# A gated tanh recurrence on TensorE: float16 split products replaced by float32 products in four column tiles

## What is computed

```python
h = silu(cond @ W1.T + b1)                       # layer 1 of the gate
gate = sigmoid(h @ W2.T + b2)[:, None, :]        # layer 2
... Haar transform of x along the steps, every coefficient times gate, inverse transform -> a
x = x + (x + a)
xW = einsum('ntd,dh->nth', x, Wx) + b
h_t = tanh(h_prev @ Wh + xW[t])                  # 256 steps in sequence, h0 = cond
x = x + h_t
```

## Time and profile before

| | before |
|---|---|
| median of 3 runs | 229.54 us (229.52 to 229.65) |
| the profiled execution | 229.55 us, of which span 227.8 us |
| PE busy | 223.4 us (98%), 3465 matmul records |
| weight loads (PEld) | 208.2 us, 3465 |
| DVE busy | 138.7 us (61%) |
| ACT busy | 108.2 us (48%) |

### The profile page before, as it was taken

The page is one execution under the profiler, slowest core; times in us unless marked ns, Lnnn a source line. Parts: engine busy times, 40 slices in busy tenths (PEclk is TensorE's granted clock), DMA queues, the critical chain, the costliest instruction groups (busy, mean ns, idle before and its releaser), DMA issues.

```text
span 227.8 us, 8577 instructions
## 1 busy us (share of the span) xinstructions
PE 223.4 (98%) x3465; PEld 208.2 (91%) x3465; DVE 138.7 (61%) x786; ACT 108.2 (48%) x773; POOL 0.5 (0%) x5
## 2 busy tenths in 40 slices
PE   7999999999999999999999999999999999999995
PEld 7899999999999999999999999999999999999984
DVE  3656666666666666666666666666666666666653
ACT  1344544455444554445544455444554445544452
POOL 0000000000000000000000000000000000000000
PEclk9999999999999999999999999999999999999999
DMA  6799930202020020202002020100202011020211
GB/s 190 219 398 415 406 140 12 86 0 98 3 92 3 3 92 4 96 3 92 3 3 94 4 95 0 77 21 4 94 3 95 0 53 45 4 94 3 95 46 49
DMA packets 6717, 18.41 MB, mean 81 GB/s; under 512 B 1171, under 2 KB 2454, under 8 KB 6678
## 3 DMA queue, kind: packets, MB, share of 16 engines
q1 hardware_dynamic: 6528, 17.71, 20.4%
q10 hardware_dynamic: 150, 0.15, 0.2%
HBM read 9.48 MB, written 8.39 MB: 78 GB/s over the span
## 4 chain that ended last, share of the span: by engine, by line
PE 97%; ACT 1%; DVE 0%; issue 0%; ACTq 0%; DVEq 0%
PE banks L241 58%; PE banks L232 33%; PE banks L221 3%; PE banks L207 2%; PE banks L215 1%; ACT L178 1%; ACT tanh_z L178 0%; ACT z L180 0%; DVE h_t L334 0%; DVE silu L359 0%; ACT h_t L198 0%; DVE ones L338 0%; DVEq L401 0%; ACTq L197 0%; ACTq L177 0%
## 5 line engine op out<-in xcount | busy, mean ns | idle before, releaser
L241 PE MATMUL banks<-h,wh_a 128*128 128x32 f16 x1530 | 132.8, 179 | 0.0
L392 DVE TENSOR_TENSOR h<-h_t,h 128x32 f16<-128x32 f32 x510 | 74.7, 188 | 81.0 <-ACT h_t L198 81.0
L232 PE MATMUL banks<-x,wx_sb 128*128 128x128 f32 x512 | 113.0, 305 | 0.0
L241 PE MATMUL banks<-h_t,wh_last 128*128 128x32 f32 x510 | 104.1, 286 | 0.0
L241 PE MATMUL banks<-h,wh_b 128*128 128x32 f16 x765 | 102.7, 176 | 0.0
L195 ACT ACTIVATE h<-banks 128x32 f16<-128x32 f32 x255 | 50.3, 197 | 110.1 <-PE banks L241 108.5
L241 PEld LDWEIGHTS banks<-h,wh_a 128*128 128x128 f16 x1530 | 86.1, 96 | 14.3
L232 PEld LDWEIGHTS banks<-x,wx_sb 128*128 128x128 f32 x512 | 75.9, 189 | 0.2 <-issue 0.2
L241 PEld LDWEIGHTS banks<-h_t,wh_last 128*128 128x128 f32 x510 | 75.8, 188 | 0.0
L241 PEld LDWEIGHTS banks<-h,wh_b 128*128 128x128 f16 x765 | 62.8, 97 | 0.0
L198 ACT ACTIVATE h_t<-banks 128x64 f32<-128x64 f32 x256 | 57.1, 223 | 0.8 <-PE banks L241 0.6
(11 more groups left out here) (33 smaller groups left out, 11.8 us busy)
## 6 DMA issues: line engine op xcount, KB each, us to landing
x<-in_x SPq DMA_DIRECT2D x15, 512.0 KB, 10.9
out_dram<-h_t SPq DMA_DIRECT2D x15, 512.0 KB, 2.6
x<-in_x SPq DMA_DIRECT2D x2, 256.0 KB, 5.0
wh_floor<-in_wh SPq DMA_DIRECT2D x1, 256.0 KB, 2.9
w_t<-in_w SPq DMA_DIRECT2D x1, 256.0 KB, 4.1
wx_sb<-in_wx SPq DMA_DIRECT2D x1, 256.0 KB, 4.9
out_dram<-h_t SPq DMA_DIRECT2D x1, 256.0 KB, 2.1
w_t<-in_w_cond SPq DMA_DIRECT2D x1, 145.0 KB, 2.6
```

What stands on the lines that cost most here:

```text
L232: return nc.tensor.matmul(pre[c % 2][e][m][:, steps, :], wx_sb[:, k, m * P:(m + 1) * P], moving, start=False, stop=False, skip_group_check ...
L241: return nc.tensor.matmul(pre[t // CS % 2][s % 2][m][:, s // 2, :], weights, h_part, start=start, stop=stop, skip_group_check=True)
L392: nc.vector.tensor_tensor(h2[:, t % 2, m, :], h_t[:, c, m, cols], h1[:, t % 2, m, :], ALU.subtract).then_inc(h2_ready[m], 1)
```

## The change

All products use PE as four tiles of 32 columns: `by_columns` cuts the 128 output columns of each weight block into four matmuls of 32 weight columns, each writing its own 32 partitions of PSUM. That holds for the gate, the bias, the input, the recurrence and the warm-ups. The recurrence is one float32 product for each of the four blocks, in the order k outside, m inside, with a wait for half k of h before each k. There are no float16 parts, no scale and nothing that computed it. ACT makes two tanhs a step, one for each half, straight into `h_t`. DVE makes no h2. A small tanh at the start loads ACT's table ahead of the gate; the gate's second layer is taken half by half, with warm-ups between; wh is loaded after wx; two bias products move behind the first input products; the last two steps are added and stored one by one.

The diff, cut to its core:

```diff
-        h1 = sb("h1", [P, 2, HALVES, B], F16)
-        h2 = sb("h2", [P, 2, HALVES, B], F16)
...
-        banks = [[ctx.enter_context(nc.psum_tensor(f"banks_{s}{e}", [P, HALVES, 512], F32)) for e in range(2)]
-                 for s in range(2)]
-        bank = [[[b[:, m, :] for m in range(HALVES)] for b in slot] for slot in banks]
+
+
+
+        bank = [[[ctx.enter_context(nc.psum_tensor(f"bank_{s}{e}{m}", [P, 512], F32)) for m in range(HALVES)]
+                 for e in range(2)] for s in range(2)]
         pre = [[[b[:, 0:N // 2].rearrange("p (s b) -> p s b", b=B) for b in parity] for parity in slot]
                for slot in bank]
 
-        scale_ps = bank[1][1][1][:, 256:257]
-        COPIES = 4
-        z_ps = [[bank[1][0][m][:, 256 + layer * P:256 + (layer + 1) * P].rearrange("p (n b) -> p n b", b=B)
-                 for m in range(HALVES)] for layer in range(2)]
+        z_ps = [[bank[1 - layer][layer][m][:, 256:256 + B] for m in range(HALVES)] for layer in range(2)]
...
-                   (CHUNKS - 1, 14, 2, T // 2)]
+                   (CHUNKS - 1, 14, 1, T // 2), (CHUNKS - 1, 15, 1, T // 2 + 1)]
...
             sp.dma_start(w1_t[:, 0, :], w1_cond[:, 0, :]).then_inc(w1_loaded[0], DMA)
-            sp.dma_start(wh_sb, wh).then_inc(wh_loaded, DMA)
             sp.dma_start(w2_t[:], w2).then_inc(w2_loaded, DMA)
             sp.dma_start(x1[:, 0, :, 0:FIRST], x[:, 0, :, 0:FIRST]).then_inc(x_first_loaded, DMA)
             sp.dma_start(wx_sb[:], wx).then_inc(wx_loaded, DMA)
+            sp.dma_start(wh_sb[:], wh).then_inc(wh_loaded, DMA)
             sp.dma_start(x1[:, 0, :, FIRST:N], x[:, 0, :, FIRST:N]).then_inc(x_loaded[0], DMA)
...
+            act.wait_ge(ones_ready, 1)
+            nc.scalar.activation(table_t[:], ones[:, 0:1], ACT.Tanh)
...
             for t in range(T):
                 c, s = t // CS, t % CS
-                z_t = banks[c % 2][s % 2][:, :, s // 2 * B:(s // 2 + 1) * B]
-                act.wait_ge(pre_ready[0], t + 1)
-                if t < T - 1:
-                    nc.scalar.activation(h1[:, t % 2, 0, :], z_t[:, 0, :], ACT.Tanh, scale=unscale_reg).then_inc(h1_ready[0], 1)
-
-                act.wait_ge(pre_ready[1], t + 1)
-                nc.scalar.activation(h_t[:, c, :, s * B:(s + 1) * B], z_t, ACT.Tanh,
-                                     scale=unscale_reg).then_inc(h_ready, 1)
-                if t < T - 1:
-                    nc.scalar.activation(h1[:, t % 2, 1, :], z_t[:, 1, :], ACT.Tanh, scale=unscale_reg).then_inc(h1_ready[1], 1)
+                for m in range(HALVES):
+                    act.wait_ge(pre_ready[m], t + 1)
+                    nc.scalar.activation(h_t[:, c, m, s * B:(s + 1) * B], pre[c % 2][s % 2][m][:, s // 2, :], ACT.Tanh)\
+                        .then_inc(h_ready[m], 1)
...
+            def by_columns(out, weights, moving, start=False, stop=False):
+                for q in range(0, P, 32):
+                    done = nc.tensor.matmul(out[q:q + 32], weights[:, q:q + 32], moving,
+                                            start=start, stop=stop, skip_group_check=True)
+                return done
...
+                return by_columns(pre[c % 2][e][m][:, steps, :], wx_sb[:, k, m * P:(m + 1) * P], moving)
...
+            def recur(t, k, m, h_part, start=False, stop=False):
+                return by_columns(pre[t // CS % 2][t % 2][m][:, t % CS // 2, :], wh_sb[:, k, m * P:(m + 1) * P], h_part,
+                                  start=start, stop=stop)
...
-            warm_up(23, bank[1][1][0])
-            gate_layer(0, w1_t, w1_t[:, :, D:D + B], z1_product, w1_loaded)
-            pe.wait_ge(small_ready, 1)
-            pe.wait_ge(largest_ready, 1)
-            nc.tensor.matmul(scale_ps, small[:], high_half(largest[:]), start=True, stop=True).then_inc(scale_product, 1)
-            warm_up(8, bank[1][1][0])
+            warm_up(22, bank[1][1][0])
+            for m in range(HALVES):
+                for k in range(HALVES):
+                    if m == 0:
+                        pe.wait_ge(w1_loaded[k], DMA)
+                    done = gate_product(0, k, m, w1_t, cond_t)
+                done.then_inc(z1_product, 1)
+            warm_up(6, bank[1][1][0])
             pe.wait_ge(w2_loaded, DMA)
-            pe.wait_ge(silu_ready, 1)
-            gate_layer(1, w2_t, silu2, z2_product, None)
+            for k in range(HALVES):
+                pe.wait_ge(silu_ready, k + 1)
+                for m in range(HALVES):
+                    done = gate_product(1, k, m, w2_t, silu2)
+                    if k == HALVES - 1:
+                        done.then_inc(z2_product, 1)
+                warm_up(3, bank[1][1][0])
             pe.wait_ge(wh_loaded, DMA)
-            pe.wait_ge(h0_ready, 1)
             for m in range(HALVES):
                 for k in range(HALVES):
-                    recur(0, m, block_of(wh_sb, k, m), h0[:, k, :], start=(k == 0))
-            pe.wait_ge(scales_ready, 2)
+                    recur(0, k, m, cond_t[:, k, :], start=(k == 0))
+            pe.wait_ge(ones_ready, 2)
             pe.wait_ge(b_ready, 2)
             lay_bias(0, 0, 0, opens=False)
             lay_bias(0, 0, 1, opens=False)
-            lay_bias(0, 1, 0)
-            lay_bias(0, 1, 1)
             pe.wait_ge(wx_loaded, DMA)
...
+            lay_bias(0, 1, 0)
+            lay_bias(0, 1, 1)
...
-                if t > 0:
-                    h1_last, h2_last = h1[:, (t - 1) % 2, :, :], h2[:, (t - 1) % 2, :, :]
-                    h_last = h_t[:, (t - 1) // CS, 1, (t - 1) % CS * B:((t - 1) % CS + 1) * B]
-
-
-                    pe.wait_ge(h1_ready[0], t)
-                    if t == 1:
-                        pe.wait_ge(wh_a_ready, 1)
-                        pe.wait_ge(wh_b_ready, 1)
-                        pe.wait_ge(wh_last_ready, 1)
+                for k in range(HALVES if t > 0 else 0):
+                    h_part = h_t[:, (t - 1) // CS, k, (t - 1) % CS * B:((t - 1) % CS + 1) * B]
+                    pe.wait_ge(h_ready[k], t)
                     for m in range(HALVES):
-                        for weights in (wh_a, wh_b):
-                            recur(t, m, block_of(weights, 0, m), h1_last[:, 0, :])
-                    pe.wait_ge(h_ready, t)
-                    recur(t, 0, wh_last[:], h_last)
-                    pe.wait_ge(h2_ready[0], t)
-                    recur(t, 0, block_of(wh_a, 0, 0), h2_last[:, 0, :], stop=True).then_inc(pre_ready[0], 1)
-                    recur(t, 1, block_of(wh_a, 0, 1), h2_last[:, 0, :])
-                    pe.wait_ge(h1_ready[1], t)
-                    for weights in (wh_a, wh_b):
-                        recur(t, 1, block_of(weights, 1, 1), h1_last[:, 1, :])
-                    pe.wait_ge(h2_ready[1], t)
-                    recur(t, 1, block_of(wh_a, 1, 1), h2_last[:, 1, :], stop=True).then_inc(pre_ready[1], 1)
+                        done = recur(t, k, m, h_part, stop=(k == HALVES - 1))
+                        if k == HALVES - 1:
+                            done.then_inc(pre_ready[m], 1)
                 fill(t)
...
-            def add_out(t):
-                c, cols = t // CS, slice(t % CS * B, (t % CS + 2) * B)
-
-                nc.vector.scalar_tensor_tensor(out=h_t[:, c, :, cols], in0=x1[:, c, :, cols], scalar=unscale[:],
-                                               in1=h_t[:, c, :, cols], op0=ALU.mult, op1=ALU.add)\
+            def add_out(t, steps=2):
+                c, cols = t // CS, slice(t % CS * B, (t % CS + steps) * B)
+                nc.vector.tensor_tensor(h_t[:, c, :, cols], h_t[:, c, :, cols], x1[:, c, :, cols], ALU.add)\
                     .then_inc(out_ready, 1)
...
+            for m in range(HALVES):
+                dve.wait_ge(tanh_z2_ready, m + 1)
+                nc.vector.tensor_scalar(g_t[:, m, :], tanh_z2[:, m, :], 0.5, 2.5, ALU.mult, ALU.add)\
+                    .then_inc(g_ready, 1)
+                dve.wait_ge(g_ready, m + 1)
+                scale(m)
+            for p in range(2, 5):
                 scale(p)
-            nc.vector.tensor_scalar(wh_last[:], wh_sb[:, SPLIT:], scale_t[:], None, ALU.mult).then_inc(wh_last_ready, 1)
-            dve.wait_ge(wh_a_ready, 1)
-            nc.vector.scalar_tensor_tensor(out=wh_b[:], in0=wh_sb[:, 0:SPLIT], scalar=scale_t[:], in1=wh_a[:],
-                                           op0=ALU.mult, op1=ALU.subtract).then_inc(wh_b_ready, 1)
-            scale(4)
 
             for t in range(T):
-                c, s = t // CS, t % CS
-                cols = slice(s * B, (s + 1) * B)
-                for m in range(HALVES if t < T - 1 else 0):
-                    dve.wait_ge(h1_ready[1] if m else h_ready, t + 1)
-                    nc.vector.tensor_tensor(h2[:, t % 2, m, :], h_t[:, c, m, cols], h1[:, t % 2, m, :],
-                                            ALU.subtract).then_inc(h2_ready[m], 1)
+
                 if t == 0:
                     scale(5)
                 elif t % 2 == 1 and (t + 11) // 2 < 8 * CHUNKS:
```

(31 more changed lines are left out.)

104 lines of the change are left out of this document (19 added, 85 removed).

## The result

| | before | changed |
|---|---|---|
| median | 229.59 us (229.52 to 229.91, 4 runs) | 322.74 us (319.24 to 327.52, 4 runs) |
| ratio | | 1.3945, 95% interval 1.3867 to 1.4023 |
| profiled execution, span | 229.55, 227.8 us | 319.24, 317.4 us |
| PE busy | 223.4 us (98%), 3465 records | 210.2 us (66%), 10808 records |
| ACT, DVE busy | 108.2, 138.7 us | 78.9, 65.7 us |

The changed kernel is 39% slower, where 16% faster was forecast. The ratio takes in only the two undisturbed runs of the changed kernel, 319.24 and 321.25 us, so it is not the ratio of the two medians.

A forecast was written before the change was run, and what follows sets the result against it. The prediction took the recurrence's loop of dependences, 0.838 us a step, to bound the kernel. It summed 10.1 + 254 x 0.70 + 2.7 = 190.6 us of span, + 1.8 = 192 us, range 168 to 258 us.

The forecast's parts named there:

- The loop of a free step: Recurrence period in a step without an instruction gap: tanh, three blocks, last matmul and ways between, forecast 0.70 us.
- B: PE's issue time for one recurrence block of four column tiles in two passes each, taken as 0.08 us.
- the lower bound: Four tiles side by side cost what one does: 54 ns for a block's two passes, period 0.63 us.
- the three blocks: Recurrence blocks k=0 m=0, k=0 m=1 and k=1 m=0, issued in turn on the loop, 0.24 us together.
- the two ways: Waits between engines: 0.03 us from a matmul's end to the tanh, 0.04 from the tanh's end to PE's weight load.
- The upper bound for B: A block's eight pairs follow at 25 ns, or 27 ns a tile: 0.20 to 0.216 us, period 1.05 to 1.09.
- rival 3: PE's instruction supply limits: 56 ns a pair, 2.2 us a step, about 583 us; chance 0.02.
- Hiding of the fill: Input and bias products on PE, 0.30 or 0.41 us with the last block, hide in a 0.47 us gap.
- Clock: PE's granted clock was forecast to hold at 1.00, the 2.4 GHz level, although PE waits in each step.
- Head: Start of the kernel: step 1's tanh at 10.1 us instead of 12.11, bounds 9.5 to 12.1.
- Tail: From the last tanh to the end of the span: 2.7 us, with a smaller addition and two last stores.
- Rivals 1, 2 and 4: Pairs 25 ns apart, 285 us (0.16); input passes serial, 249 us (0.14); better tile overlap, under 171 us (0.02).

The follow-up runs named there:

- e4_tiles64: The changed kernel with two tiles of 64 columns in place of four of 32; measured 230.6 us in the profiled run, 236.1 in the other.

## Why the prediction was wrong, point by point

**The loop of a free step: right.** Forecast 0.70 us, measured 0.72. B was put at 0.08 and is 0.06, nearly the lower bound: tiles start 7 ns apart and one pass of four every 32 ns. From the end of the last matmul to the tanh it is 0.07, not 0.03, and from the tanh to PE 0.05, not 0.04. So part of the close hit is luck: the three blocks were put 0.03 too long and the two ways 0.05 too short, and the errors nearly cancel. The forms of 64 and 128 columns, expected at 0.82 and 1.14 by the same sum with the measured ways, gave 0.84 and 1.15. The upper bound for B, pairs 25 ns apart, does not hold between tiles: 7 ns here. The Trainium skill gives such a floor of 25 ns from start to start on the page "TensorE: Matmul & The Clock Gate", section "Wait — 56ns, not 53.3ns?"; the trace differs between column tiles. The 4 ns between neighbouring tiles that the Trainium skill gives on the same page, Part 3, are near the 7 measured.

**The step that failed is rival 3, "PE's instruction supply".** Its mechanism was the right one and it got a chance of 0.02, on the argument that the kernel before waits for h, not for instructions. That argument shows that supply was enough at 26 instructions a step and says nothing of 80. Its price, 56 ns a pair, was the rate at which that kernel used instructions, not one at which they come: measured are 3.6 us for 128 pairs, 28 ns. With this, and with 41 pairs a step (bias products make one a step on average), the sum would have been 10.1 + 254 x 41 x 0.028 + 2.7 + 1.8 = 306 us, and with four blocks held up by the x loads for 2.4 us each about 316, against 319 to 328 measured. The change's tripling of PE's instructions was counted in the prediction (13 pairs to 40), but weighed only as PE time. The page of before had the row to start from, q8 with 27 packets for 0.44 MB, 16 KB apiece; how soon the next packet could follow, it does not show. So nothing there spoke for 0.02, and the price was open.

**Hiding of the fill: right, while instructions last.** Input and bias products lie between the last recurrent pair and the tanh's result, and the free period is 0.72 us in the last seven steps too, which have none.

**Clock: wrong.** It did not hold. The mean is 0.954, with 0.53 from 8.3 to 10.3 us, once PE had been busy 0.2 of the 2.6 us before, and 0.53 from 18 to 30 us, where it was busy 6.3 of 12. The stretches of the head answer to the earlier trace rows:

```profile
5.70:8.30 2.60, 0.19 (x16) 0.03 (x4) 1.72 (x8) 0.46 (x2) 0.00 (x0) 1.00 0.61 213
8.30:10.30 2.00, 2.00 (x64) 1.95 (x68) 0.49 (x2) 0.09 (x1) 0.00 (x0) 0.53 0.51 93
10.30:12.30 2.00, 2.00 (x56) 1.93 (x52) 0.29 (x1) 0.31 (x2) 0.00 (x0) 0.62 0.99 391
...
18.00:30.00 12.00, 6.28 (x256) 5.07 (x256) 1.48 (x6) 1.83 (x12) 0.00 (x0) 0.53 1.01 405
```

**Head: wrong, 12.9 us instead of 10.1 for the second tanh of step 1.** This answers to the earlier trace rows:

```profile
8.28 0.60 PE L158 MATMUL bank<-w_t,wh_sb 128*32 128x32 f32 x32 [2.41 <-DMA wh_sb<-in_wh]
...
8.86 1.70 PEld L158 LDWEIGHTS bank<-x,wx_sb 128*32 128x32 f32 x32
...
12.27 0.46 PEld L158 LDWEIGHTS bank<-h_t,wh_sb 128*32 128x32 f32 x31
...
12.83 0.29 ACT L149 ACTIVATE h_t<-bank 128x32 f32<-128x32 f32 x2 [1.56 <-PE bank L158]
```

wh landed at 8.28, not 7.7 (issued at 2.81 us, 5.4 to land). The 32 pairs of four input products then took 1.70 us at the lower clock, and four more products and two bias products another 1.3 and 0.4. The table load did leave the path; by itself it is worth 0.4% on the kernel before, with the doubt said above.

**Tail: off by 0.8 us.** From the first tanh of step 255 (313.77) to the end of the span are 3.6 us, where 2.7 were counted from the second, 0.1 later. Three stores queue on SP at the end.

**Rivals 1, 2 and 4: out.** No 25 ns spacing, no row of eight input pairs at 108 ns (eight start within 0.18 us), and no free step under 0.62 us.

## What to carry to other kernels

Before cutting products into small tiles, count instructions, not only columns: in these runs PE waits for the next block wherever it would go through 256 instructions in less than about 3.6 us, whatever the products cost; that is 14 ns an instruction. Wider tiles need fewer: here 64 columns do the step in 0.84 us with 40 instructions, no faster than before, and 32 columns would do it in 0.72 us with 80, which are not delivered in time. And the low use of a resource (27 packets, 8 us apart) is only a lower bound on what it can carry, and no reason to give its exhaustion a small chance when the change triples the use.

## What the runs showed of the hardware

- PE's instruction blocks of 16 KB started 3.57 to 3.64 us apart on average between 100 and 200 us, at four different counts a step and mean clocks from 0.84 to 0.95 (single ones 3.3 to 4.1 in the changed kernel after 45 us). From the start of a packet to PE's next instruction it was 2.3 to 3.0 us, of which 0.9 to 1.4 is the packet, and from there to the start of the next packet 1.1. While x loaded at about 400 GB/s they were 6 us apart. The page "Runtime: NRT & Kernel Launch" of the Trainium skill, Instruction fetch mechanics, says that crossing a block is mostly hidden because the sequencer is slower than the fetch; the trace differs, PE goes through 256 instructions in 2.2 us between two gaps.
- Four tiles of 32 columns take float32 passes at 7 ns from tile to tile, 32 ns for the four; two tiles of 64 take 58 ns for the two (e4_tiles64).
- Two changes of tile width a step cost 0.09 us with both at the fill, 0.15 with one of them on the loop. From the last pair of 32 columns to the first of 64 or of 128 it was 0.13 us in both runs.
- The granted clock fell to 0.50 in a kernel whose PE records were 100% busy (float32 products with 128 weight columns and 32 moving ones) and stayed at 1.00 with the same products in two tiles of 64.
